# An attention and router kernel whose y stays channels by tokens up to the last stage: softmax sums from columns of ones, spread by DMAs

## The reference

```
qkv = x @ w_attn.T;  32 heads of 16;  rope on q and k
y = softmax(causal(q k.T / sqrt(16))) v
y = y + gating * softmax(q ak.T / sqrt(512)) av      # ak, av: 10 adapter rows
x = layernorm(x + y @ w_proj.T)
base = x @ base_w.T + base_b;  hidden = x @ A.T;  probs = softmax(x @ router_w.T), 16 experts
combine = the two largest probs, divided by their sum
x = layernorm(x + base + 0.5 * sum_e combine_e (hidden @ B_e.T))
```

## Time and profile before

| | us |
|---|---|
| three timed runs: median (lowest to highest) | 876.29 (875.12 to 880.50) |
| span of the profiled execution, first to last instruction | 874.7 |
| PE busy in that span | 855.2 |
| DVE busy | 721.0 |
| ACT busy | 470.5 |
| POOL busy | 236.7 |

### The profile page before, as it was taken

How to read it: one execution, slowest core, us unless ns; L and a number is a source line. 1 busy time by engine, 2 the same in 40 slices (tenths; PEclk the granted TensorE clock), 3 DMA queues, 4 the chain that set the end, 5 groups by cost and what they waited for, 6 DMA issues and landing times.

```text
span 874.7 us, 15938 instructions
## 1 busy us (share of the span) xinstructions
PE 855.2 (98%) x5386; PEld 551.8 (63%) x5386; DVE 721.0 (82%) x2228; ACT 470.5 (54%) x1040; POOL 236.7 (27%) x277
## 2 busy tenths in 40 slices
PE   9999999999999999999999999999999999999996
PEld 6788867785444444444444454444468888888885
DVE  4865667779999999999999999995676777777766
ACT  4333313223788888888888888888742121212110
POOL 0222220222222333323333336333332222222221
PEclk9999999999999999999999999999999999999999
DMA  7316180727133331133442253313010010101011
GB/s 271 121 49 193 61 230 24 218 80 182 34 74 75 75 75 42 35 74 75 75 75 47 34 118 75 74 52 101 30 37 25 25 48 24 48 24 48 25 36 37
DMA packets 32402, 66.61 MB, mean 76 GB/s; under 512 B 5772, under 2 KB 7244, under 8 KB 32332
## 3 DMA queue, kind: packets, MB, share of 16 engines
q1 hardware_dynamic: 32332, 65.72, 29.4%
HBM read 44.11 MB, written 20.97 MB: 74 GB/s over the span
## 4 chain that ended last, share of the span: by engine, by line
PE 81%; DVE 8%; issue 3%; ACT 2%; DMA 1%; POOL 1%; SPq 1%; DVEq 0%; POOLq 0%; ACTq 0%
PE bank L1644 16%; PE bank L1512 16%; PE bank L448 11%; PE bank L1520 11%; PE bank L450 10%; PE bank L449 10%; PE bank L1626 2%; PE bank L1457 2%; DVE bank L1070 2%; PE bank L1473 1%; DVE xtl L1195 1%; ACT xth L874 1%; DVE mx L1073 1%; PE bank L1720 1%; DMA ks<-k_parts 1%
## 5 line engine op out<-in xcount | busy, mean ns | idle before, releaser
L920 ACT ACTIVATE pt<-bank 128x512 f32<-128x512 f32 (+3 forms) x768 | 325.8, 496 | 67.9 <-PE bank L1512 61.4
L1070 DVE CUSTOM_DVE_ANT_0 bank<-bank,cmask 128x512 f32<-128x512 f32 (+3 forms) x512 | 234.3, 527 | 9.2 <-PE bank L1520 6.4
L1512 PE MATMUL bank<-qs,ks 50*128 50x512 f32 (+3 forms) x768 | 216.2, 397 | 0.4 <-ACT pt L920 0.2
L1512 PEld LDWEIGHTS bank<-qs,ks 50*128 50x128 f32 x768 | 109.3, 184 | 136.0 <-ACT pt L920 117.6
L1073 DVE TENSOR_REDUCE mx<-bank 128x1 f32<-128x512 f32 x256 | 160.8, 687 | 9.8 <-PE bank L1520 8.4
L1644 PE MATMUL bank<-pt,vb 128*32 128x512 f32 (+3 forms) x1536 | 163.4, 498 | 0.8 <-POOL pt L701 0.8
L1520 PE MATMUL bank<-ks,qs 48*128 48x512 f32 (+3 forms) x768 | 161.2, 385 | 2.8 <-DVE mx L1070 1.3
L701 POOL TENSOR_SCALAR_AFFINE_SELECT pt<-pt 128x512 f32<-128x512 f32 x128 | 81.5, 638 | 284.3 <-ACT pt L920 284.3
L1520 PEld LDWEIGHTS bank<-ks,qs 48*128 48x128 f32 x768 | 90.6, 185 | 33.5 <-DVE mx L1070 11.2
L644 POOL TENSOR_TENSOR part<-rope,part 128x1024 fp32r<-128x1024 f32 x16 | 38.2, 2386 | 165.0 <-ACT part L768 165.0
L874 ACT CAST xth<-bank 128x512 fp32r<-128x512 f32 x15 | 8.8, 586 | 135.0 <-PE bank L1720 135.0
(11 more groups left out here) (196 smaller groups left out, 1441.1 us busy)
## 6 DMA issues: line engine op xcount, KB each, us to landing
qs<-q_parts SPq DMA_DIRECT2D x34, 256.0 KB, 4.0
ks<-k_parts SPq DMA_DIRECT2D x34, 256.0 KB, 6.9
q_parts<-part SPq DMA_DIRECT2D x32, 256.0 KB, 3.4
k_parts<-part SPq DMA_DIRECT2D x32, 256.0 KB, 3.6
qs<-q_parts SPq DMA_DIRECT2D x34, 128.0 KB, 5.0
ks<-k_parts SPq DMA_DIRECT2D x34, 128.0 KB, 5.9
vb<-in_x SPq DMA_DIRECT2D x16, 256.0 KB, 2.7
out<-outb SPq DMA_DIRECT2D x16, 256.0 KB, 2.0
```

The costliest lines, as they stand in the source:

```text
L920: act.activation(pt[k % PT_BUFS][:, h, 0:width(st)], half(n % SCORE_BUFS)[:, 0:width(st)], ACT.Exp, scale=float(HD) ** -0.5).then_inc(S("e ...
L1070: last = ve.tensor_tensor_reduce(blk, blk, cmask[:, BANK - nk * P:], 1.0, NEG, ALU.add, ALU.max, mx[m][:, 0, h, qt:qt + 1])
L1512: pe.matmul(half(n % SCORE_BUFS)[:, 0:q1 - q0], ks[slot_of(g)][r0:r0 + KX, h // 2, kb * P:(kb + 1) * P], qs[slot_of(g)][r0:r0 + KX, h // 2 ...
```

## The change

- `y_all` is now [channels, chunk of 128 channels, tokens]. The adapter's matmuls swap their operands so that their output is channels by tokens too.
- `vb` has 16 columns of ones instead of one of ones and 15 of zeros, and there are two such buffers instead of three.
- `trans_out`, the copy into `yrow`, `t_y`, `tile_y`, `hi_y` and `lo_y` go. The maxima keep the four banks to themselves.
- After both halves of `yts` are written, SP issues eight DMAs (`move_y`): one row of sums per head into `den` (a row of 1024 as 32 partitions by 32), and 16 rows of y per head into `yv`. DVE inverts `den` (128x32) once per group, at chunk 22 of the next group. SP writes the inverse to DRAM, waits, and loads it back with four DMAs, each spread over 16 partitions (`spread_den`).
- For two groups, which fill the 128 partitions of `yv`, POOL multiplies and adds in two halves of 512 tokens (`divide`, in every second group; the last pair in round 3 of the tiles).
- POOL writes the high and low halves of each tile of y directly from `y_all` (`split_y`), two tiles ahead.
- ACT's copies into `yts` wait for the DMAs of the group before.

```diff
+INVERT_AT = 22
+DIVIDE_STEPS = [9, 11]
...
-        y_all = sb(ctx, "y_all", [P, G, QT, HG * HD])
+        y_all = sb(ctx, "y_all", [P, CC, NB * T])
...
+            def move_y(g):
+                r0 = HALF * (g % 2)
+                sp.wait_ge(S("y_copied"), 2 * (g + 1))
+                if g > 0:
+                    sp.wait_ge(S("den_inverted"), g)
+                if g >= 2:
+                    sp.wait_ge(S("y_added"), HEAD["y_added"] + 2 * (g // 2))
+                for h in range(HG):
+                    sp.dma_start(den[VW * h:VW * h + VW], yts[VW * h + HD:VW * h + HD + 1].rearrange("o (a b) -> o a b", b=T // 32)
+                                 ).then_inc(S("y_moved"), 16)
+                for h in range(HG):
+                    sp.dma_start(yv[r0 + HD * h:r0 + HD * h + HD], yts[VW * h:VW * h + HD]).then_inc(S("y_moved"), 16)
+
+            def spread_den(g):
+                r0 = HALF * (g % 2)
+                sp.wait_ge(S("den_inverted"), g + 1)
+                if g >= 2:
+                    sp.wait_ge(S("den_spread"), 16 * HG * (g - 1))
+                sp.dma_start(dens[g % 2].rearrange("h (a b) -> (h a) b", b=T // 32), rden[:]).then_inc(S("den_stored"), 16)
+                sp.wait_ge(S("den_stored"), 16 * (g + 1))
+                for h in range(HG):
+                    sp.dma_start(rspread[r0 + HD * h:r0 + HD * h + HD], dens[g % 2, h].partition_broadcast(HD)
+                                 ).then_inc(S("den_spread"), 16)
...
+                if g > 0:
+                    move_y(g - 1)
+                    spread_den(g - 1)
                 if g + 1 < G:
                     store_max(g + 1, use_of(g, ROWS_AT))
...
             sp.dma_start(bias[:], d["base_b"].partition_broadcast(P)).then_inc(S("bias_ld"), 16)
+            move_y(G - 1)
             def sp_c(j, m):
+                if isinstance(j, int) and j == 2:
+                    spread_den(G - 1)
...
+            def divide(k, i):
+                g, n = 2 * k + 1, 2 * k + i
+                q0 = i * BANK
+                gp.wait_ge(S("den_spread"), 16 * HG * (g + 1))
+                gp.wait_ge(S("y_added"), HEAD["y_added"] + n)
+                gp.tensor_tensor(yv[:, q0:q0 + BANK], yv[:, q0:q0 + BANK], rspread[:, q0:q0 + BANK], ALU.mult
+                                 ).then_inc(S("y_divided"), 1)
+                gp.wait_ge(S("y_divided"), n + 1)
+                t0 = (k // CC) * T + q0
+                ydst = y_all[:, k % CC, t0:t0 + BANK]
+                gp.tensor_tensor(ydst, ydst, yv[:, q0:q0 + BANK], ALU.add).then_inc(S("y_added"), 1)
...
+            def split_y(t, m):
+                if isinstance(t, int) and t == 0:
+                    gp.wait_ge(S("y_added"), HEAD["y_added"] + 2 * CC)
+                    gp.wait_ge(S("score_full"), (G - 2) * SCORE_BANKS)
+                if ahead(t - 1):
+                    gp.wait_ge(S("proj_full"), t - 1)
+                    apart(gp, t)
+                src = y_all[:, :, bass.ds(t * P, P)]
+                gp.tensor_copy(yth[m], src).then_inc(S("y_high"), 1)
+                gp.wait_ge(S("y_high"), t + 1)
+                apart(gp, t)
+                gp.tensor_tensor(ytl[m], src, yth[m], ALU.subtract).then_inc(S("y_low"), 1)
...
                 act.wait_ge(S("pv_done"), NS * g + LAST_STEP[i] + 1)
                 if g > 0:
-                    act.wait_ge(S("max_full"), norm_use(g - 1, i) + 1)
+                    act.wait_ge(S("y_moved"), 16 * 2 * HG * g)
                 act.copy(yts[:, i * BANK:(i + 1) * BANK], values_out).then_inc(S("y_copied"), 1)
...
+            def invert(g):
+                ve.wait_ge(S("y_moved"), 16 * 2 * HG * (g + 1))
                 if g > 0:
+                    ve.wait_ge(S("den_stored"), 16 * g)
+                ve.reciprocal(rden[:], den[:]).then_inc(S("den_inverted"), 1)
...
+                    if slot == FIRST[INVERT_AT] and g > 0:
+                        invert(g - 1)
...
-                    last = pe.matmul(out[:, i * P:(i + 1) * P], pat[a_ % 2][:, i], avbd[:, i], start=True, stop=True)
+                    last = pe.matmul(out[:, i * P:(i + 1) * P], avbd[:, i], pat[a_ % 2][:, i], start=True, stop=True)
```

More of the change, by code:

```diff
@@ L172 @@
     USE0.append(USE0[-1] + sum(held(_g, n) for n in range(SLOTS)))
-MAX_TOTAL = USE0[G] + 1
+MAX_TOTAL = USE0[G]
 def use_of(g, slot):
     return USE0[g] + sum(held(g, n) for n in range(slot))
[L181 to L193, removed]
 NTC = NB * QT
@@ L735, in gp_c @@
                     add_bias(j - 1, 1 - m)
-                if isinstance(j, int) and j == 1:
-                    normalise(G - 1, 1)
+                if isinstance(j, int) and j == 3:
+                    divide(CHUNKS - 1, 0)
+                    divide(CHUNKS - 1, 1)
+                    gp.wait_ge(S("y_added"), HEAD["y_added"] + 2 * CHUNKS)
+                if not isinstance(j, int) or 2 <= j < NTC - 2:
+                    split_y(j + 2, m)
             drive_tiles(gp, gp_c)
@@ L940, in act_c @@
                 if not sure and j == 2:
-                    hi_y(3, 1)
                     hi_g(0)
@@ L1145, in ve_group @@
                         max_rows(g + 1, use_of(g, slot))
-                    if slot - NORM_LAG in NORM_AT and held(g, slot - NORM_LAG):
-                        back, i = NORM_OF[NORM_AT.index(slot - NORM_LAG)]
-                        invert(g + back, i)
-                    if slot in NORM_AT or not held(g, slot):
+                    if slot == FIRST[INVERT_AT] and g > 0:
+                        invert(g - 1)
+                    if not held(g, slot):
                         continue
@@ L1617, in _ @@
             trans_rows(0, NMX)
-            def trans_out(g, i):
-                q0, nq = NORM[i]
-                pe.wait_ge(S("y_copied"), 2 * g + 1 + i)
-                if (g, i) == (G - 1, 1):
-                    pe.wait_ge(S("x1_low"), 1)
-                out = free_bank(norm_use(g, i))
-                for q in range(nq):
-                    last = pe.transpose(out[:, q * P:(q + 1) * P], yts[:, (q0 + q) * P:(q0 + q + 1) * P], ident[:])
-                last.then_inc(S("max_full"), 1)
             def weighted(g, st):
@@ L1687, in _ @@
             keep_on(half(SCORE_BUFS - 1))
-            def t_y(t, m):
-                pe.wait_ge(S("y_tile"), t + 1)
-                if isinstance(t, int) and t == 0:
-                    pe.wait_ge(S("max_read"), reads_before(MAX_TOTAL))
-                    pe.wait_ge(S("out_copied"), len(NORM) * (G - 1) - 1)
-                if ahead(t):
-                    pe.wait_ge(S("y_low"), t)
-                for c_ in range(CC):
-                    last = pe.transpose(half(Y_BANK)[:, c_ * P:(c_ + 1) * P], ytile[m][:, c_ * P:(c_ + 1) * P], ident[:])
-                last.then_inc(S("y_transposed"), 1)
             def proj(t, m, parts=range(CC)):
@@ L1815, in pe_c @@
                     ar(j - 1, 1 - m)
-                if not sure and j == 1:
-                    trans_out(G - 1, 1)
                 if sure or 3 <= j < NTC - 1:
```

205 lines of the change are left out of this document (51 added, 154 removed).

## The result

The changed kernel took 988.35 us in the median of 4 runs (973.8 to 1000.54), the kernel before 877.79 beside it: a ratio of 1.114 (95% interval 1.106 to 1.122). Every ratio here is taken over the runs within 1.5% of the fastest of their kernel, so it isn't that of the medians. Some 11% slower, against the -0.6% forecast. The execution profiled took 982.75, with a span of 980.9; its counterpart is the span of 874.7.

A forecast was written before the change was run, and what follows sets the result against it. It took attention to be bound by a loop of DVE and PE, with DVE nearly full. Attention -6.4, group 11 +2.3, last group -2.6, transition +1.3, tiles 0 made -5.4 us: 871 us, range 862 to 886.

The forecast's parts named there:

- The step that failed: Attention: y's DMAs land 0.6 us before DVE asks for them at its reciprocal, so nothing was added for waiting.
- Issue: Attention: SP issues the eight DMAs at 0.47 us each, the last 3.3 us after ACT's second copy ends.
- Landing: Attention: the DMAs land 1.7 us after issue, at 330.4, with bounds of 329.6 and 333.0.
- The first rival: Attention: DVE's reciprocal waits for late DMAs in every group; typically 886 us, 899 if landing at 333.0; chance 0.20.
- The gain of 0.46 us a group: Attention: DVE's 0.45 us wait for PE goes and two reciprocals become one; 6.4 us over 14 groups.
- the third rival: Attention: no gain, since ACT's banks hold PE's half of the loop and DVE's wait stays; 877 us; chance 0.18.
- Group 11: Attention, one group: y's DMAs queue behind 1 MB of weights and DVE waits; 2.3 us slower.
- Last group: Last attention group: PE sets the pace and loses five transpositions; 2.6 us faster, between 1 and 3.
- Transition: Last group to tiles: the reciprocal waits for eight DMAs, delaying the weight remainder; 1.3 us slower, between 0.5 and 4.
- Tiles: Last stage: the removed y transposes lay inside PE's wait for x's low half; tile stays 14.5 us, nothing gained.
- The second rival: Last stage: the tiles give their transposes back, 12 x 0.6 = 7.2 us more gain, 864 us; chance 0.12.

The follow-up runs named there:

- e4: Kernel before plus the change's eight DMAs, to scratch nobody reads, with DVE and ACT waiting for them in groups 2 to 14: 953.06 us, ratio 1.084.
- e2: Changed kernel with a separate semaphore for the den DMAs and two alternating y buffers, so nothing waits on them too early: 949.77 us, ratio 1.064.
- e6: Kernel before with one transpose instead of four in each half of every group but the last two, result incomplete: 936.76 us.
- e5: e2 plus two unread TensorE products of 512 columns, at chunks 30 and 35 of groups 1 to 14: 898.69 us, ratio 1.021.
- e12: As e11, but with one unread product of 512 columns at chunk 30 and none at chunk 35: 875.33 us, ratio 0.995.
- e7: e4 without DVE's wait for the DMAs; ACT's copy still waits: 943.53 us.
- e9: Kernel before, no DMA of the change, with two extra unread DVE operations ahead of chunk 22's pair in groups 2 to 14: 986.25 us.
- e10: Changed kernel, its waits kept, plus two unread TensorE products of 512 columns at chunks 30 and 35 of groups 1 to 14: 976.62 us.
- e1: Changed kernel with one column of ones and 15 of zeros in V, as the kernel before has: 991.18 us, ratio 1.128.
- e11: e5 with products of 256 columns, w_projT's load behind the y DMAs, and another order behind the last group: 873.1 us, ratio 0.997.
- e8: Kernel before, no DMA of the change, with one extra unread DVE operation ahead of chunk 22's pair in groups 2 to 14: 890.47 us, ratio 1.016.

## Why the prediction was wrong

**The step that failed** is the one in which landing decides between "DVE asks" and "DVE waits", and above all what follows from it. I priced a late landing as the time by which DVE waits, one for one, and the loss of PE work as nothing or a gain. No term of the sum and no rival had the granted clock in it, though the rows showed 1.00 in each window and PE's row at 26.09 of 26.10 us. I read that full row as a bound; the work behind it was also what held the clock, and the kernel's own `keep_on` products in group 0, whose result nobody reads, should have made me ask for it.

- *Issue.* 0.47 us was taken from the loads; it is 0.59 each and the next starts 0.63 later, eight in 5.0 us (247.36 to 252.37). That is the row of the maxima's DMAs, 0.64, which I had only as the bound and for four of them. The last is issued 4.4 us after the copy's end, not 3.3.
- *Landing.* 2.3 us after issue instead of 1.7, so 13.0 to 14.0 us into the groups that come there at full clock, against 11.26 forecast and 12.0 asked. My bounds, 10.5 to 13.9, held all but the two latest of these, which were less than 0.1 us over. The about 2.0 us of the Trainium skill (DMA: Bandwidth & Descriptors, the section on the anatomy of one DMA) was nearer, though that section gives it for DMAs issued by GpSimd and these are SP's. With the issue as measured neither 1.7 nor 2.0 would have left a margin: 12.4 and 12.7 us into the group.
- *The first rival* had the mechanism's beginning right and its size wrong. With landing at 13.0 to 14.0 its own working gives 887 to 901. e4's group at full clock confirms the price: 1.17 us for waits of 1.0 and 0.9. The falls of the clock were left out of it, and they are nearly all of the loss: 260 us more at the lower level x 0.38 = 99 us of the 106 between the two spans. The 0.38 comes from e2's groups 5 and 6, and e6's groups 6 and 7 give 0.40 (4.04 us for 10.2), so this is an estimate: 99 to 104 us, and the remaining 2 to 7 are waits, less what the other parts gave.
- *The gain of 0.46 us a group* did not come. At full clock e2's group takes 26.05 against 26.09. DVE's wait at the sixth score stayed at 0.45 us, and PE's freed time became a wait of 0.33 us for ACT at chunk 30: the third rival, that PE's half of the loop is held by ACT's banks, was right here. Taking six of eight transposes away in e6 brought 0.17 us.
- *Group 11.* 2.3 forecast; with nothing else late (e5) PE stood for 2.66 us and the clock fell during that stop; together 6.4 us over its neighbours.
- *Last group.* From its first score to the last copy of y 33.9 us against 36.0: -2.1, forecast -2.6.
- *Transition.* Forecast +1.3. From the last copy of y to the transposes of tile 2: 18.2 us before, 23.3 after, +5.1. DVE's and PE's timeline there:

```profile
754.17 0.35 DVE L1115 RECIPROCAL rden<-den 128x32 f32<-128x32 f32 x1 [5.55 <-DMA yv<-yts]
754.44 2.23 DVE L1155 TENSOR_TENSOR wbl<-v_all,ks 128x2048 fp32r<-128x2048 f32 x1
...
762.09 0.80 PE L422 MATMUL bank<-wbh,ks 128*128 128x512 f32 x1 [5.71 <-DVE ks L1166]
```

  The remainder starts 8.6 us after the last copy of y does, against about 6 forecast (4.15 before); PE stands for 5.71 us instead of 0.99, and from 758.4 on, inside this stop, the clock is at 0.50 for 6.8 us. The term went wrong by the same issue time and more of it: the four den DMAs took 3.44 us here. That the remainder is faster without POOL beside it was right, and it gave back 0.71 us (2.23 against 2.94), not 0.4. In e12, where DVE inverts later, the same stretch takes 17.4 us.
- *Tiles.* Forecast 14.5, nothing gained; measured 14.36 against 14.53. Hidden they were, but for 0.17 us a tile. The second rival (13.9 a tile) was wrong.

So of the sum, each part outside attention came out within 4 us. In attention the gain was not there, and the cost was of a kind that I had not listed.

How the clock fell can be told from rows. In groups 1 to 14 of the kernel before with its transposes, stops of PE up to 0.98 us left it at 2.4 GHz, and those of 1.1 us and more came with a fall to 1.2 GHz (e4, e7, e9). Group 0 is an exception: there it fell in e4 and e9 with no stop over 0.18 us. With other work in place of the transposes (e10) 0.68 us could do it and 0.97 did not, so the stop's length alone doesn't decide. With the transposes' work missing no stop over 0.34 us was needed (e2), and in e6 none at all. The Trainium skill (TensorE: Matmul & The Clock Gate, the section on a second failure mode) tells of a kernel in which TensorE idles briefly but often between groups of matmuls, so that its clock swings between the two levels. The clock swings between the two levels in e2 and e6 as well, but frequent idling is not in their rows: one stop of 0.33 us ahead of a fall in e2, and 0.08 us of idle time in 19.45 in e6. What exactly is counted, no run here shows.

## What to carry to other kernels

When a change takes work from a TensorE that is full and at full clock, ask first what keeps the clock up, and put a price on its fall: here each microsecond at the lower level cost some 0.4, and a stop 1 us longer cost a group 7.6. A product in the code whose result nobody reads is a hint that this was needed before. Look at the granted clock by windows before any wait; a busy row does not show it. Where work must go, put something into the hole (one product of 512 columns a group, which cost 0.1 us), and do not hang two engines on a chain of eight DMAs whose landing moved by 1 us from group to group.

## What the runs showed of the hardware

- In the group shown a DMA from SBUF to SBUF issued by SP took 0.59 us of the queue and the next began 0.63 later, whether it moved 64 KB or 4 KB (behind the last group four of 4 KB took 3.44); 64 KB landed 2.3 us after issue, the 4 KB ones, spread from one partition over 32, 3.3 (median of the group shown).
- The falls lasted 3 to 38 us, and 51 in e1, e6 and e11; a stop of 0.45 to 0.57 us brought none in the twelve groups of e8, one of 1.3 to 2.1 us brought one in each of the groups 2 to 14 of e9.
- Removing work from the busiest engine, with no wait added anywhere, made the kernel before 2.5 to 8% slower in four runs (898.54 to 948.79, against 876.22 in the median).
- Stops of TensorE of the same length, 1.70 to 1.72 us in e9, were followed by falls of 3.4 us in four groups and of 17.1 to 20.5 us in seven others.
